# Attention: the value products of four key tiles in one block on TensorE, in place of two

## What is computed

```
q, k, v = split(h @ w_qkv + b_qkv)           # 16 heads, 32 channels each
q, k = rope(q), rope(k)
attn = softmax(q @ k.T * (1 / sqrt(32)))     # over 2048 keys
out  = attn @ v                              # then @ w_ao + b_ao, residual, norm, feed-forward
```

## Time and profile before

| | us |
|---|---|
| median of 3 runs | 3211.46 (3205.74 to 3218.61) |
| the profiled execution | 3215.83 |
| its span, first to last instruction | 3214.0 |
| PE busy | 3078.1 (96%) |
| DVE busy | 1866.1 (58%) |
| ACT busy | 1539.9 (48%) |
| POOL busy | 1676.0 (52%) |
| mean granted TensorE clock | 0.979 of full speed |

### The profile page before, as it was taken

How to read it: one execution, slowest core, us unless ns; L and a number is a source line. 1 busy time by engine, 2 the same in 40 slices (tenths; PEclk the granted TensorE clock), 3 DMA queues, 4 the chain that set the end, 5 groups by cost and what they waited for, 6 DMA issues and landing times.

```text
span 3214.0 us, 39670 instructions
## 1 busy us (share of the span) xinstructions
PE 3078.1 (96%) x15073; PEld 2084.2 (65%) x15073; DVE 1866.1 (58%) x2975; ACT 1539.9 (48%) x2823; POOL 1676.0 (52%) x709
## 2 busy tenths in 40 slices
PE   6999999999999999999999989799999999999999
PEld 6777754555555555554555544478888888888887
DVE  3558777878878788787887876443333333222222
ACT  2333266767767677676776767532223222111111
POOL 3455568888888888888888878621121100000000
PEclk9899999999999999999999999899999999999999
DMA  4665479998998989989899897632222201121110
GB/s 170 188 184 161 130 180 187 191 190 184 198 190 186 196 186 199 192 185 194 179 200 193 178 204 163 150 124 79 79 79 79 73 11 50 53 92 66 53 53 27
DMA packets 171749, 455.88 MB, mean 142 GB/s; under 512 B 23956, under 2 KB 57832, under 8 KB 140136
## 3 DMA queue, kind: packets, MB, share of 16 engines
q0 software_dynamic: 32256, 234.90, 36.8%
q1 hardware_dynamic: 137624, 213.21, 22.8%
q10 hardware_dynamic: 1680, 5.24, 0.4%
HBM read 139.77 MB, written 78.64 MB: 68 GB/s over the span
## 4 chain that ended last, share of the span: by engine, by line
PE 43%; POOL 23%; DMA 21%; issue 8%; DVE 3%; ACT 1%; SPq 0%; POOLq 0%; DVEq 0%; ACTq 0%
DMA b_pt<-b_pt 19%; POOL b_acc L811 17%; PE e_a L1425 11%; PE e_g L1425 10%; PE e_y L1435 10%; POOL b_acc L799 3%; PE e_p L1370 2%; PE b_s L896 2%; PE b_o L944 2%; POOL a_q_lo L326 2%; PE a_qk L478 1%; PE b_m L880 1%; POOL a_yq L319 1%; DMA b_qs<-scratch_qk_lo 1%; PE a_c L446 1%
## 5 line engine op out<-in xcount | busy, mean ns | idle before, releaser
L828 DVE TENSOR_REDUCE b_mpart<-b_m 128x1 f32<-128x512 f32 x1960 | 1200.0, 680 | 327.6 <-PE b_m L880 327.3
L779 ACT ACTIVATE b_pt<-b_s 128x512 f32<-128x512 f32 x2048 | 1088.1, 602 | 427.4 <-PE b_s L896 385.2
L811 POOL TENSOR_TENSOR b_acc<-b_acc,b_pt 128x2048 f32<-128x2048 f32 x224 | 1043.7, 4659 | 228.7 <-DMA b_pt<-b_pt 228.0
L896 PE MATMUL b_s<-b_qs,b_ks 98*128 98x512 f32 x2048 | 858.6, 421 | 50.5 <-ACT b_pt L779 25.4
L880 PE MATMUL b_m<-b_ks,b_qs 96*128 96x512 f32 x1960 | 760.0, 408 | 0.0
L896 PEld LDWEIGHTS b_s<-b_qs,b_ks 98*128 98x128 f32 x2048 | 391.9, 192 | 383.3 <-issue 191.9
L944 PE MATMUL b_o<-b_pt,b_vg 128*32 128x512 f32 x4096 | 504.4, 611 | 0.0
L880 PEld LDWEIGHTS b_m<-b_ks,b_qs 96*128 96x128 f32 x1960 | 374.7, 191 | 125.1 <-DVE b_mpart L828 52.9
L1307 DVE SCALAR_TENSOR_TENSOR e_u_lo_f<-e_a,keep_chan,e_u_lo_f 128x512 f32<-128x512 f32 x128 | 96.0, 750 | 539.9 <-PE e_a L1425 539.6
L1425 PE MATMUL e_g<-e_h_hi,e_w 128*128 128x512 f32 x1024 | 340.0, 393 | 26.6 <-DVE e_w_lo L1299 18.3
L1425 PE MATMUL e_a<-e_h_hi,e_w 128*128 128x512 f32 x1024 | 337.8, 391 | 0.0
(11 more groups left out here) (130 smaller groups left out, 3016.1 us busy)
## 6 DMA issues: line engine op xcount, KB each, us to landing
b_pt<-b_pt POOLq DMA_DIRECT2D x224, 1024.0 KB, 8.4
scratch_qk_hi<-a_q_hi SPq DMA_DIRECT2D x64, 256.0 KB
scratch_qk_lo<-a_q_lo SPq DMA_DIRECT2D x64, 256.0 KB
b_qs<-scratch_qk_hi SPq DMA_DIRECT2D x64, 256.0 KB, 6.3
b_ks<-scratch_qk_hi SPq DMA_DIRECT2D x28, 512.0 KB, 6.0
scratch_v<-a_vsb SPq DMA_DIRECT2D x32, 256.0 KB, 2.7
b_qs<-scratch_qk_lo SPq DMA_DIRECT2D x32, 256.0 KB, 8.2
b_vg<-scratch_v SPq DMA_DIRECT2D x16, 512.0 KB, 5.1
```

Of the source, the lines that this page charges most:

```text
L779: act.activation(pt[:, kt % RING, h, :], ps_s[:, score_place(i) % LEAD, :], ACT.Exp, scale=SCALE).then_inc(p_ready, 1)
L811: pool.tensor_tensor(acc[u % 2][:], acc[u % 2][:], pt[:, (2 * n + 3) % RING, :, :], ALU.add).then_inc(pool_added, 1)
L828: dve.tensor_reduce(mpart[n % 2][:, i // 4, i % 4:i % 4 + 1], ps_m[:, at, :], AX.X, ALU.max).then_inc(max_done, 1)
L896: pe.matmul(ps_s[:, place % LEAD, :], ks[n // NJ % 2][0:QR, h, kt * P:(kt + 1) * P], qs[n % 4][0:QR, h, :], start=True, stop=True).then_in ...
```

## The change

The value products come after every fourth tile, four tiles together, where they came after every second, two together. Nothing else differs: the same matmuls, the same waits in front of each, the same rings and banks.

```
-                if kt % 2 == 1:
-                    if kt == 1:
+                if kt % 4 == 3:
+                    if kt == 3:
                         pe.wait_ge(o_read, u + 1)
                         if u % NJ == 0:
                             pe.wait_ge(v_in[u // NJ % 2], 32 * (u // NJ // 2 + 1))
-                    for n in (kt - 1, kt):
+                    for n in range(kt - 3, kt + 1):
                         pe.wait_ge(p_ready, STEPS * (u + 1) + GH * (n + 1))
                         for h in range(GH):
                             last = pe.matmul(ps_o[h * HD:(h + 1) * HD, 0, :], ...
```

## The result

The changed kernel takes 3475.09 us (median of 4 runs, 3469.93 to 3480.67), the kernel before 3213.43 us (four runs too, 3205.74 to 3218.61): 1.081 times as long, 95% interval 1.078 to 1.083, 262 us more. The direction was forecast, the size was not: 137 us were, with 3410 as the upper end.

A forecast was written before the change was run, and what follows sets the result against it. The loop of POOL and DMA was taken to bound the kernel; fold 1's 5.2 us wait less 0.8 of landing is 4.4 a unit, over 31 units 136 us on 3215.8, 3352, as median 3348; range 3260 to 3410.

The forecast's parts named there:

- What bounds the kernel: In attention, mostly the loop of POOL and DMA sets the pace, 50.0 us a unit, though PE is 96% busy.
- Fold 1 waits: On POOL, fold 1 is issued 5.2 us after add 6, not at once; a unit grows by 4.4 us.
- Rival 3: The loop as forecast, but PE's clock falls more often: fold 1 waits 1.3 us more a unit, 3388 us; chance 0.15.
- I charge nothing for them: Folds 3 and 5 on POOL get products later but stand behind adds 1 and 3: nothing, 1 us a unit at most.
- The landings: Fold 1's transfer starts after fold 0 has landed, so it lands 0.8 us sooner, between nothing and 1.5, from 8.4.
- The sum: 31 units grow by 4.4 us each, 136 us on the profiled 3215.8, giving 3352; as median of runs 3348.
- What it does to DVE: DVE's gap behind a block grows to 2.6 us, four kt take 12.3 us, a unit 51.1 without the loop.
- term of 1.8 us: In DVE's unit, the denominators' matmuls and small instructions on the maximum: the middle between 0 and 3.4 us.
- rival 2: The loop absorbs the wait and DVE sets the pace: 1.1 us more a unit, 35 us, 3246; chance 0.16.
- PE's saving: Each pair of joined blocks saves PE 0.34 us, 43 us in all; if PE sets the pace 3168, chance 0.05.
- The order on SP's queue: The piece of keys waiting for the sixth tile goes out two kt later: costs nothing, 41 us if late.

The follow-up runs named there:

- the four kernels of the table: Kernel before, changed kernel, changed kernel with a maxima matmul done 20 times, changed kernel with query loads issued later: units of 49.9, 59.2, 57.0, 55.9 us.
- the copies: Changed kernel, with the maxima matmul before the score matmul that waits for ACT at kt 7 done 20 times over: 3418.92 us, 1.065.
- the joints at 11 and 15: Two runs, kernel before with only tiles 8 to 11, or only tiles 12 to 15, multiplied as one block: 3346.88 us and 3359.54 us.
- joined at 3 only: Kernel before with only tiles 0 to 3 multiplied as one block, all others in twos: 3210.46 us, 0.999.

## Why the prediction was wrong

**What bounds the kernel: right.** With POOL's work cut, a unit takes 48.4 us and not 50, and in the four kernels of the table the odd folds' waits, their landings and the adds behind them follow each other without slack and add up to the unit.

**Fold 1 waits: right in kind, and the step whose size failed first.** The step was "fold 1 is issued 3.1 + 1.8 + 0.3 = 5.2 us after add 6". Measured: 7.8 on average. With the copies it was 5.2 in the unit shown and 5.7 on average; the other 2.1 us are PE at half rate in the seven matmuls and the first half of the block. On average the block now began 4.3 us after add 6 and fold 1 followed 3.5 us later; with the copies, in the units with 5.2 us, these are 3.0 and 2.3, where 3.1 and 2.1 were forecast. The forecast took its 3.1 from a unit in which PE had idled 1.37 us, and the time of the half block from one at full clock; now PE idles 2.9 to 5.55 us before them, in each of units 2 to 28. Rival 3 held this mechanism, at 1.3 us a unit and a chance of 0.15; its sign was a clock under 0.93 over the stretch, and 0.93 is what was measured. It belonged in the forecast: the wait that the change adds is itself the idle time that lowers the clock.

**"I charge nothing for them" (folds 3 and 5): wrong.** They waited 1.0 and 0.3 us, 1.3 in a unit; the range had 1. That the joints at 11 and 15 cost 129 and 142 us each when alone shows how thin that cover was: the forecast had fold 3 and its products ready at the same moment, 18 us after add 6. PE's low clock isn't the reason, since with the copies these waits stayed at 1.1 and 0.3 us. There the block of kt 11 began 17.3 us after add 6, where 16 was reckoned; why so late was not looked into further.

**The landings: half right.** Fold 1 lands 0.9 us sooner, as taken (0.8). That folds 3 and 5 would land 0.4 and 1.5 us later was in no step. Fold 5 used to be issued before the unit's border and now goes out beside the query loads; moving these took its landing from 10.1 to 7.3 us. The 8.4 us of the earlier trace rows was a median over all folds, and I applied it to transfers that the change moves in time.

**The sum.** Forecast 5.2 - 0.8 = 4.4 a unit. Measured 9.3: 7.6 more wait before fold 1, 0.9 less for its landing, 1.3 for the waits of folds 3 and 5, 1.9 for their landings, and 0.5 less in the rest, which makes 9.4 with rounding. Over 31 units 4.4 is 136 us and 9.3 is 288; 262 were measured, since the first unit didn't grow (47.6 us, where it was 49.3) and nor did unit 29, already long before (56.7, where it was 60.1). By size, the terms that failed are the wait before fold 1 (2.6 us over its 5.2), the landings of folds 3 and 5 (1.9, put at nothing) and their waits (1.3, put at nothing).

**What it does to DVE: right.** Forecast were a gap of 2.6 us, 12.3 us for four kt and a unit of 51.1 where POOL doesn't bind; measured 2.68, 12.33 and 50.9. The 51.1 holds a term of 1.8 us that was the middle between 0 and 3.4, so its closeness is in part luck. The gap is time in which DVE has no new maxima to read; it grew with the block, 0.95 to 2.68 us. Of rival 2 it was the mechanism, but the loop ends later.

**PE's saving: right in sign, too large.** 43 us were forecast for a PE that sets the pace, 12 measured. The block of four is 3.5 to 3.6 us as forecast (3.6; 1230.42 to 1233.88 in the unit shown, and 3.57 in the block before it), but a joint saved 0.19 us at best and not 0.34 (11.39 us for four kt, against 2 x 5.79), and in stretches with the denominators or the turned maxima the blocks were further apart. Which of ACT's pace and PE's own order takes the rest was not tried apart.

**The order on SP's queue: cost nothing found.** With products joined at 3 only, where that piece keeps its time, and at 7, the difference is accounted for by fold 1's wait; it was not tried alone.

## What to carry to other kernels

When products are gathered into larger blocks, ask who waits for the product that comes late by it, and follow that waiter's queue round until it comes back: if the block itself waits for the end of that loop, the whole distance is added to each turn, whatever is saved on the engine. Price such a new wait with the clock that its own idle time leaves, and price each transfer on it by what runs beside it at its new time, not by the median. A joint whose late product stands in no loop was free here, and also brought nothing; and where the loop was out of the way, blocks of four still cost 79 us, because VectorE had nothing to read during each.

## What the runs showed of the hardware

The 1 MB accumulating transfer inside SBUF landed in 6.9 us with nothing beside it (fold 0 of the changed kernel, issued at 1550.25). Beside the query loads it took 10.1 us on average (fold 5 there), and 11.3 us beside these and fold 5 (fold 6). PE's granted clock was 0.56 of full over 8.8 us after an idle time of 5.55 us; with 20 repeated matmuls in that wait, which left 0.85 us of it idle in the unit shown, the mean of the span was 0.980. VectorE added 128 x 2048 float32 in 2.50 us on average, where POOL took 4.7 in the same kernel.
